# Attention: transposed queries behind three of four probability transposes; last layer: stream joined at each batch's beginning, output in halves

## The reference

```python
def _layer(x, wqkv, qs, ksc, wo, lg, lb, w1, b1, w2, b2):
    h = shift_token(x)
    q, k, v = split(h @ wqkv, 3)                  # 8 heads of 64
    q = l2norm(q) * qs ; k = l2norm(k) * ksc
    q, k = rotary_xpos(q, k)
    o = local_attention(q, k, v)                  # windows of 128, each looks at itself and the one before
    x = x + o @ wo
    h = layernorm(shift_token(x)) * lg + lb
    a, g = split(h @ w1 + b1, 2)                  # 682 wide each
    return x + (a * gelu(g)) @ w2 + b2
...
x = x + _L0_ffn_ref(_layernorm(x), ...)           # two such layers, then the sum
```

## Time and profile before

| | |
|---|---|
| median of 3 timed runs | 1042.76 us (1042.3 to 1044.64) |
| the profiled execution, its own time | 1037.41 us |
| its span, first to last instruction | 1035.7 us |
| mean granted TensorE clock | 0.984 |
| busy: PE, PEld | 953.1 us, 767.3 us |
| busy: DVE, ACT, POOL | 668.4, 514.0, 411.5 us |
| attention of layer 0, of layer 1 | about 398 to 606, 721 to 928 |
| feed-forward of the last layer | about 928 to 1029 |

### The profile page before, as it was taken

How to read it: one execution, slowest core, us unless ns; L and a number is a source line. 1 busy time by engine, 2 the same in 40 slices (tenths; PEclk the granted TensorE clock), 3 DMA queues, 4 the chain that set the end, 5 groups by cost and what they waited for, 6 DMA issues and landing times.

```text
span 1035.7 us, 17394 instructions
## 1 busy us (share of the span) xinstructions
PE 953.1 (92%) x5656; PEld 767.3 (74%) x5656; DVE 668.4 (65%) x1686; ACT 514.0 (50%) x1217; POOL 411.5 (40%) x416
## 2 busy tenths in 40 slices
PE   5889969999999988999999889999999999889987
PEld 4668855767676866878787777887787878678876
DVE  6878476357574687666666645577766666645663
ACT  4577731403021325666666554454766666654432
POOL 4233613113120347666666410006675767620030
PEclk9899989999999998999999999999999999999999
DMA  6201013000000000000001020000000000000002
GB/s 244 72 1 61 21 41 107 1 1 1 0 0 1 1 22 1 1 22 0 21 0 30 13 94 20 4 6 20 1 23 0 21 0 18 20 15 17 11 0 85
DMA packets 15172, 26.32 MB, mean 25 GB/s; under 512 B 1098, under 2 KB 11712, under 8 KB 14352
## 3 DMA queue, kind: packets, MB, share of 16 engines
q1 hardware_dynamic: 15120, 25.68, 7.6%
HBM read 20.53 MB, written 2.10 MB: 22 GB/s over the span
## 4 chain that ended last, share of the span: by engine, by line
PE 70%; DVE 9%; ACT 8%; issue 6%; POOL 4%; SPq 2%; DMA 1%; POOLq 0%; ACTq 0%; DVEq 0%
PE bank L1528 30%; PE bank L1862 5%; PE bank L1675 5%; PE bank L1817 5%; PE bank L1723 5%; PE bank L1841 4%; PE bank L1827 4%; ACT probs L1393 4%; PE bank L1804 2%; PE bank L1852 2%; SPq L335 1%; PE bank L1686 1%; POOL scanned L402 1%; PE bank L1594 1%; PE bank L1936 1%
## 5 line engine op out<-in xcount | busy, mean ns | idle before, releaser
L1393 ACT ACTIVATE probs<-bank,row_min 128x256 f32<-128x256 f32 (+1 forms) x256 | 111.6, 462 | 120.8 <-DVE row_min L987 120.8
L534 POOL TENSOR_TENSOR norms<-norms,minus_half 128x16 f32<-128x16 f32 x32 | 93.6, 2924 | 2.7
L987 DVE CUSTOM_DVE_ANT_0 bank<-bank,mask 128x256 f32<-128x256 f32 (+1 forms) x256 | 90.7, 425 | 5.7 <-PE bank L1817 5.6
L1528 PE MATMUL bank<-wqkv_hi,x_hi 128*128 128x512 f32 x192 | 82.6, 430 | 1.8 <-DVE rot L963 1.1
L1528 PE MATMUL bank<-wqkv_lo,x_hi 128*128 128x512 f32 x192 | 76.5, 398 | 0.0
L1528 PE MATMUL bank<-wqkv_hi,x_lo 128*128 128x512 f32 x192 | 76.0, 396 | 0.0
L1124 DVE SCALAR_TENSOR_TENSOR hidden<-bank,lcols,hidden 128x512 f32<-128x512 f32 (+1 forms) x48 | 36.0, 749 | 51.0 <-PE bank L1528 28.3
L1827 PE MATMUL bank<-ident,probs 128*128 128x128 f32 x448 | 61.6, 279 | 3.7 <-ACT probs L1393 3.7
L516 POOL TENSOR_TENSOR q_tok<-rot 128x512 f32<-128x512 f32 x32 | 41.1, 1286 | 57.7 <-DVE rot L963 57.7
L1528 PE MATMUL bank<-t_hi,wm_hi 128*128 128x512 f32 x160 | 63.6, 397 | 0.0
L1528 PE MATMUL bank<-t_lo,wm_hi 128*128 128x512 f32 x160 | 63.6, 397 | 0.0
(11 more groups left out here) (239 smaller groups left out, 2680.2 us busy)
## 6 DMA issues: line engine op xcount, KB each, us to landing
w_stage<-in_wm_l_dram SPq DMA_DIRECT2D x8, 534.0 KB, 3.6
w_stage<-in_wqkv_dram SPq DMA_DIRECT2D x2, 1536.0 KB, 7.7
out_dram<-stream SPq DMA_DIRECT2D x4, 512.0 KB, 3.7
emb<-in_ctx_dram SPq DMA_DIRECT2D x1, 1536.0 KB, 6.9
inner<-in_w_gate_dram SPq DMA_DIRECT2D x1, 1152.0 KB, 10.3
stream<-in_x_dram SPq DMA_DIRECT2D x2, 512.0 KB, 5.8
stream<-in_x_dram SPq DMA_DIRECT2D x1, 1024.0 KB, 12.7
ew<-in_pos_bias_dram SPq DMA_DIRECT2D x1, 1024.0 KB, 11.2
```

The source lines that it names most:

```text
L534: pool.tensor_tensor(norms[:, 2, :], norms[:, 1, :], minus_half[:, :], ALU.pow).then_inc(c_rn, 1)
L987: dve.tensor_tensor_reduce(logits, logits, mask[:, 2 * P - nk:2 * P], 1.0, FAR, ALU.add, ALU.min, row_min[:, w % 2, 2 * i + e:2 * i + e + ...
L1393: act.activation(probs[:, i, e, 0:nk], logits, ACT.Exp, bias=row_min[:, w % 2, h:h + 1], scale=-1.0, accum_out=row_sum[:, w % 2, h:h + 1]) ...
L1528: ins = pe.matmul(out, stationary, moving, start=(first and i == 0), stop=(last and i == len(terms) - 1))
```

## The change

In attention, PE and ACT have the third set of the probabilities ahead of the queries instead of behind them. In the last layer, POOL adds `inner` (which then holds attention's result) to `stream` at each batch's beginning, each add followed by the next batch's `mlp_rstd`; DVE adds the down product to `stream` instead of `inner`, half by half, after a wait on POOL's add; and SP stores each half on its own, batch 0 and 1 between the stacking DMAs of the later batches.

```diff
@@ sync
+            def store(b):
+
+                for h, done, before in ((0, d_res0, NB * (LAYERS - 1)), (1, b_res, NB * LAYERS)):
+                    half = slice(b * TT + 2 * h, b * TT + 2 * h + 2)
+                    sp.wait_ge(done, before + b + 1)
+                    sp.dma_start(ov[:, half, :], stream[:, half, :]).then_inc(out_sem, 16)
...
                 for b in range(NB - 2, NB):
+                    if l == LAYERS - 1:
+                        store(b - 2)
                     stack_last(l * NB + b)
-            for b in range(NB):
-                sp.wait_ge(out_sum, b + 1)
-                sp.dma_start(ov[:, b * TT:(b + 1) * TT, :], stream[:, b * TT:(b + 1) * TT, :]).then_inc(out_sem, 16)
-            sp.wait_ge(out_sem, 16 * NB)
+            for b in range(NB - 2, NB):
+                store(b)
+            sp.wait_ge(out_sem, 32 * NB)
@@ gpsimd
-                with pool.Fori(0, NB - 1) as b:
-                    mlp_rstd(l * NB + b + 1)
                 if l < LAYERS - 1:
+                    with pool.Fori(0, NB - 1) as b:
+                        mlp_rstd(l * NB + b + 1)
...
+            pool.wait_ge(c_res, NT * LAYERS)
             for b in range(NB):
 
-                pool.wait_ge(b_res, NB * LAYERS + b + 1)
+                pool.wait_ge(b_res, NB * LAYERS + b)
                 pool.tensor_tensor(stream[:, tiles(b), :], stream[:, tiles(b), :], inner[:, tiles(b), :], ALU.add)\
                     .then_inc(out_sum, 1)
+                if b < NB - 1:
+                    mlp_rstd((LAYERS - 1) * NB + b + 1)
@@ vector, mlp
-                    s = inner[:, bass.ds(b * TT + 2 * h, 2), :]
+                    s = (inner if l < LAYERS - 1 else stream)[:, bass.ds(b * TT + 2 * h, 2), :]
+                    if l == LAYERS - 1:
+                        dve.wait_ge(out_sum, b + 1)
@@ scalar, window
-                probs_transposed(n, w, 0)
+                for i in range(KI - 1):
+                    probs_transposed(n, w, i)
                 if one:
                     queries(n + 1)
-                probs_transposed(n, w, 1)
-                probs_transposed(n, w, 2)
-                probs_transposed(n, w, 3)
+                probs_transposed(n, w, KI - 1)
@@ tensor, window
-                transpose_probs(n, w, 0)
-                transpose_probs(n, w, 1)
+                for i in range(KI - 1):
+                    transpose_probs(n, w, i)
                 if one:
                     transpose_q(n + 1, (w + 1) % 2)
-                transpose_probs(n, w, 2)
-                transpose_probs(n, w, 3)
+                transpose_probs(n, w, KI - 1)
```

## The result

The changed kernel takes 1027.58 us, the median of 4 runs (1023.85 to 1028.41), against 1042.53 us (1039.86 to 1044.64, 4 runs) for the kernel before beside it. The ratio is 0.9851, 95% interval 0.9829 to 0.9873: faster by 15.0 us between medians. The profiled execution takes 1023.85 us, its span 1022.0 us, 13.7 us less than before's 1035.7; its mean granted clock is 0.987, before's 0.984.

The account below looks back on a forecast made before the run. PE, busy 92% of the 1035.7 us span, was taken as the bound. Attention 7.6, batch 2's stall 2.9 and the tail 3.1 sum to 13.6 us, so 1042.76 - 13.6 = 1029.2 us, range 1026.5 to 1036.0.

Parts of the forecast that it names:

- Attention, 7.6 us forecast: Attention windows of both layers: probability transposes fill PE's wait before the query transposes, 8.4 us won less 0.8 lost.
- The last window but one: One window a layer: the output projection waits for the later query copy, 0.4 us each, 0.8 in two layers.
- ACT reaches it only behind copy 2: Last window but one: ACT finishes the third probability copy near 586.95, then copies queries until 587.55; projection 0.4 us late.
- the rival in which products or the value copy take the gap's place: Attention: PE waits there instead, so attention gives half or nothing, 1033 or 1036.8 us; chance 0.13 for half or more.
- rooms of 0.4 us and more: Attention window: PE's value projection keeps 0.4 to 0.55 us of room behind DVE's products, the x transpose about the same.
- The room of the query copy: Attention window: the delayed query copy ends at 494.05, the output projection needs it at 494.97, leaving 0.9 us.
- in the ordinary window the delay costs nothing: Attention's ordinary windows: the query copy, behind two more copies on ACT, still precedes the output projection; no cost.
- The stall of batch 2: Last feed-forward: moving POOL's adds away from DVE's `hidden_lo` subtractions removes 2.9 us, bounds 2.0 to 3.0.
- The four adds at their new places: Last feed-forward, batch beginnings: POOL's adds there hold up no DVE instruction and cost nothing.
- The tail: Kernel end: dropping POOL's last add saves 2.4 us and halving the last store 0.75; 3.1 taken, bounds 2.4 to 3.7.
- The median: Whole kernel: timed median stands 5.35 us above the profiled execution, and the saving carries over unchanged.

Follow-up runs that it names:

- e3: Changed kernel with ACT's query copy back behind the first probability copy, PE's order kept new: 1025.75 us, ratio 0.9845.
- e10: Changed kernel with all four probability sets ahead of the queries on PE, ACT's query copy behind the first probability copy: 1024.5 us, ratio 0.982.
- e11: As e10, but each layer's last window but one keeps the order of the kernel before: 1024.81 us, ratio 0.9821.
- e4: Changed kernel with all four probability sets ahead of the queries on both PE and ACT: 1027.81 us, ratio 0.986.
- e5: Kernel before with only POOL's adds of the last layer's batches 0 to 2 made earlier: 1039.88 us, ratio 0.9965.
- e9: Changed kernel with POOL's four adds replaced by one-element memsets, so the output is incomplete: 1028.64 us, one run.
- e6: Changed kernel with each batch stored whole (512 KB, one DMA) instead of in halves: 1026.69 us, one run.
- e1: Kernel before with only the attention reordering on PE and ACT, last layer as before: 1034.2 us, ratio 0.9911.

## Why the prediction was right

The prediction said 1029.2 us, 13.6 less. Spans moved by 13.7 and medians by 15.0.

**Attention, 7.6 us forecast, 7.44 measured** within the two layers, scores to scores. The 7.57 at the last window hold 0.22 already there at the first scores, which no term had, less 0.09 lost between the layers. Kind by kind: third and fourth windows gave 0.24, not the 0.26 of the gap (2.9 for 3.1). Second windows gave all of the 0.44 (13.59 to 13.15), first ones 0.22, as worked out (3.5 and 1.3). The two very first gave 0.53 and 0.20, 0.7 for 0.5. That is 8.4 in all, as forecast, from terms that missed by 0.2 in either direction. That they met so closely is in part luck: layer 0's very first window took 15.29 to 15.62 us in the traces with before's order and 14.99 to 15.60 in those with more sets ahead, and before's was its longest.

**The last window but one, 2 x 0.4 forecast, 0.34 and 0.61 measured.** That the projection would wait for a late query copy was right. The reason given, that ACT reaches it only behind copy 2, holds in layer 1 alone and for a third of the loss. In layer 0, from which it was reckoned, ACT stood idle 0.26 us until the query transposes were done (row at 582.17), so the copy was late because PE's transposes were; e3 leaves the loss whole there and 0.4 us of it in layer 1. The size was taken from a window at half the clock and applied to both layers. Before, layer 1's window ran at full clock and took 12.19 us, layer 0's 13.68. At full clock PE reaches the projection earlier (the weight loads of its last set take 0.47 us, against 0.84 in layer 0) while the copy keeps its 0.60, so the same reordering costs more: 0.61. Together 0.95 us, for 0.8.

**The gap doesn't move.** In a third and a fourth window after's PE is busy 13.34 of 13.34 and 13.36 of 13.36 us, so the rival in which products or the value copy take the gap's place is out. The reason given, rooms of 0.4 us and more, is not contradicted by any run: in e10 and e11 first windows get 0.22 us shorter still.

**The room of the query copy was read from one window and given to all.** 0.9 us was reckoned, and a fourth window has 0.84. A second window has 0.63, and 0.43 in the last batches. Nothing in this change needed the difference; one more copy, in e4, did. The step "in the ordinary window the delay costs nothing" was true with less to spare than it said.

**The stall of batch 2, 2.9 forecast, 2.88 measured** (27.96 to 25.08), alone in e5 too. The four adds at their new places: nothing forecast, nothing found (e9).

**The tail, 3.1 forecast, 3.25 measured.** The add's removal gives 2.4, as the row had it, and the store's size 0.8 (e6) where 0.75 was taken from the stretches at the end. The tail itself says 0.8, the median time to landing 0.6 (3.0 against 2.4). The Trainium skill's figure for the bytes ("DMA: Bandwidth & Descriptors", "Anatomy of one DMA — SWDGE (gpsimd) path") gave 0.6 too, and the trace agrees with it in that view.

**The median.** The prediction carried 1042.76 - 1037.41 = 5.35 us over "for reasons the profile doesn't show". The list of runs, each with span and mean granted clock, shows a part of the reason. Runs of the kernel before, seen beside all experiments: at clock 0.983, 1039.84 to 1040.38 us; at 0.981, 1040.62 to 1042.97; at 0.978, 1044.46 to 1045.63; at 0.976, 1046.55; the profiled one had 0.984 and 1037.41. So 0.001 of clock goes with about 1 us, and up to 2.4 us of spread is left at one clock. After: 0.982, 1028.38 and 1028.41; 0.983, 1026.78; 0.987, 1023.85. At 0.983 the two kernels lie at 1040.1 and 1026.78, 13.3 us apart, near the 13.7 of the spans, though from one run of after. The rest between the medians may be after's higher clock; that isn't shown, as the clocks of before's runs beside it aren't on record. Kernels with both parts of the change had 0.980 to 0.988, those with one part 0.977 to 0.983, before 0.976 to 0.984. Whether the change raises the clock (it shortens PE's idle times) or these executions had it by chance stays open. Part of the spread is one window. In e1's layer 1 the last window but one ran at half the clock throughout, and in before's layer 1 it didn't. The stretches of 10 us ahead of each one's key transposes, and of 5 us from there (e1's two, then before's two), and the transposes themselves:

```profile
889.47:899.47 10.00, 6.94 (x65) 5.48 (x63) 7.38 (x28) 5.18 (x19) 6.91 (x7) 0.95 0.05 13
899.47:904.47 5.00, 5.00 (x24) 4.95 (x24) 0.49 (x5) 3.21 (x7) 3.18 (x5) 0.50 0.08 22
...
899.47 1.09 PE L1795 MATMUL bank<-ident,k_tok 128*128 128x128 f32 x4 [3.06 <-DVE k_tok L978]
900.35 2.77 PE L1826 MATMUL bank<-ident,probs 128*128 128x128 f32 x12
```

```profile
895.94:905.94 10.00, 6.95 (x64) 5.48 (x63) 6.96 (x28) 5.13 (x19) 6.50 (x6) 1.00 0.05 14
905.94:910.94 5.00, 5.00 (x36) 4.33 (x38) 0.73 (x6) 3.50 (x8) 3.18 (x5) 1.00 0.08 22
...
905.94 0.63 PE L1796 MATMUL bank<-ident,k_tok 128*128 128x128 f32 x4 [3.06 <-DVE k_tok L978]
906.40 1.04 PE L1827 MATMUL bank<-ident,probs 128*128 128x128 f32 x8
```

Behind the length and five busy times stands PEclk: in the 5 us from the transposes on 0.50 (1.2 GHz) in e1 against 1.00 (2.4 GHz) in before. PE had done the same before it, 6.94 and 6.95 us of 10, and idled the same 3.06; the clock fell within that idle time, at about 898.5, 1 us before the transposes, and hence the 0.95 of e1's first stretch. It was full again at 905.3. The twelve probability transposes take 2.77 us, where after's take 1.47 at full clock, and the window 14.97 us instead of 12.80.

## What to carry to other kernels

Work that an in-order engine has ready belongs ahead of its wait, up to the length of the gap; the gain is then the smaller of the two, window kind by window kind. Before moving a copy back in a queue, read the room of its first reader in every kind of window, the one with the least work in between above all. An add that joins two tensors at the end of a program can often be made before the last term exists, beside instructions that read PSUM; and before comparing two executions whole, look at their granted clocks and compare stage by stage.

## What was unexpected of the hardware

- With the same 3.06 us of PE idle and the same work in the 10 us up to its end, the granted clock of the next 5 us was 1.00 in one execution (before) and 0.50 in another (e1), where it had fallen 1 us before the idle ended. With the new order the window takes 12.80 us at full clock (after) and 14.97 at half (e1). Across executions of the kernel before, a mean clock of 0.976 to 0.983 goes with 1046.55 down to 1039.84 us.
- A DVE subtraction beside a POOL add lost 1.34 us of the 1.46 they shared. In all three cases read, it ended 0.55 to 0.56 us behind the add, though it takes 0.68 by itself. The second of before's adds was lengthened too, 2.84 us for 2.36. A POOL memset of 0.95 us, shared for 0.5 us, cost the pair nothing.
- A half store landed in 2.4 us, a whole one in 3.0 to 3.2 (e6), but in 2.9 to 5.1 in the kernel before, whose stores are all issued in the last 25 us.
